# Eight scatters a sequence, each held until its predecessor has landed and five of them ahead of the first normalisation's GpSimd step

## The reference, cut to what matters

```python
x = x + L0_xattn(layernorm(x), ctx, ctx)      # 16 heads of 16, Wq Wk Wv Wo bo
x = x + L0_ffn(layernorm(x))                  # 16 experts, 4 a token, shared expert
x = x + L1_xattn(layernorm(x), ctx, mask)     # q k v with biases, masked keys
x = x + L1_ffn(layernorm(x))                  # 16 experts, 2 a token, shared expert
# L0_ffn of an input x (normalised):
scores = sigmoid(x @ gate_w.T)                # 4 experts of the 2 best groups of 4
y = sum over chosen e of cw[e] * (silu(x @ Wg[e].T) * (x @ Wu[e].T)) @ Wd[e].T
return x + y + shared(x)
```

## Time and profile before

| | us |
|---|---|
| median of three runs | 2772.32 |
| lowest and highest run | 2769.62 and 2779.53 |
| span of the profiled execution | 3211.6 |
| TensorE busy in it | 2501.5 (78%) |
| vector engine busy | 1619.2 (50%) |
| ScalarE busy | 1173.3 (37%) |
| GpSimd busy | 998.9 (31%) |

### The profile page before, as it was taken

How to read it: one execution, slowest core, us unless ns; L and a number is a source line. 1 busy time by engine, 2 the same in 40 slices (tenths; PEclk the granted TensorE clock), 3 DMA queues, 4 the chain that set the end, 5 groups by cost and what they waited for, 6 DMA issues and landing times.

```text
span 3211.6 us, 52941 instructions
## 1 busy us (share of the span) xinstructions
PE 2501.5 (78%) x16160; PEld 1935.5 (60%) x16161; DVE 1619.2 (50%) x5230; ACT 1173.3 (37%) x2564; POOL 998.9 (31%) x1104
## 2 busy tenths in 40 slices
PE   6888888888897499999768787788788877699400
PEld 4667676667676387778545565555556655587400
DVE  2655555556565344444336555455455545344333
ACT  3444444445353133333234434334343443233100
POOL 1232333332323500000134434434443442400366
PEclk9998989999898799999889889889898889899755
DMA  4111111111111544444431212211221120544465
GB/s 163 43 64 42 58 47 57 49 63 42 63 43 55 138 151 148 148 150 149 133 108 60 71 64 62 70 61 60 63 70 55 60 76 33 136 149 148 144 178 171
DMA packets 202635, 292.72 MB, mean 91 GB/s; under 512 B 30423, under 2 KB 151514, under 8 KB 202074
## 3 DMA queue, kind: packets, MB, share of 16 engines
q1 hardware_dynamic: 160522, 185.09, 18.0%
q0 software_dynamic: 37456, 102.81, 10.2%
q10 hardware_dynamic: 4608, 4.20, 0.9%
HBM read 155.65 MB, written 136.34 MB: 91 GB/s over the span
## 4 chain that ended last, share of the span: by engine, by line
PE 54%; another core or an unknown queue 12%; DVE 10%; issue 9%; ACT 8%; POOL 4%; DMA 3%; SPq 0%; DVEq 0%; POOLq 0%; ACTq 0%
PE ps L1358 12%; PE ps L1293 7%; PE ps L1366 6%; PE ps L1212 5%; PE ps L1193 4%; PE ps L1233 3%; ACT W L667 3%; POOL ygath L543 3%; PE ps L1371 3%; PE ps L1176 2%; DVE mxp L846 2%; PE ps L1281 2%; PE ps L1268 2%; PE ps L1377 1%
## 5 line engine op out<-in xcount | busy, mean ns | idle before, releaser
L510 POOL DMA_INDIRECT xsort<-xn,xidx x384 | 377.7, 984 | 570.7 <-DVE xidx L1050 467.8
L846 DVE TENSOR_REDUCE mxp<-ps 128x8 f32<-128x960 f32 x256 | 284.6, 1154 | 498.2 <-PE ps L1212 268.3
L1358 PE MATMUL ps<-wgu,ygath 128*128 x1664 | 440.6, 387 | 28.0 <-issue 23.3
L543 POOL DMA_INDIRECT ygath<-ysort,yidx x384 | 371.2, 967 | 152.3 <-issue 107.6
L1212 PE MATMUL ps<-KB,Q 64*128 64x240 f32 x2048 | 287.5, 428 | 100.7 <-DVE mxp L846 80.3
L1100 DVE TENSOR_TENSOR ygath<-ygath,ps 128x128 f32<-128x128 f32 x416 | 119.5, 287 | 441.6 <-ACT ygath L744 441.6
L667 ACT ACTIVATE W<-ps 120x1024 f32<-120x1024 f32 x256 | 249.6, 1034 | 239.8 <-remote 169.8
L1358 PEld LDWEIGHTS ps<-wgu,ygath 128*128 128x128 f32 x1664 | 284.9, 191 | 74.2 <-issue 52.2
L1212 PEld LDWEIGHTS ps<-KB,Q 64*128 64x128 f32 x2048 | 218.3, 218 | 165.7 <-DVE mxp L846 86.9
L1293 PE MATMUL ps<-W,wsgu 128*128 128x256 f32 x1024 | 290.7, 434 | 1.2 <-ACT th L691 1.2
L1193 PE MATMUL ps<-xnT,wq 128*128 128x256 f32 x1024 | 280.0, 422 | 10.8 <-ACT xnT L630 9.3
(11 more groups left out here) (160 smaller groups left out, 4027.9 us busy)
## 6 DMA issues: line engine op xcount, KB each, us to landing
ygath<-xsort SPq DMA_DIRECT2D x416, 128.0 KB, 2.0
ysort<-ygath SPq DMA_DIRECT2D x208, 256.0 KB, 2.3
based<-XO SPq DMA_DIRECT2D x64, 256.0 KB
XB<-in_x SPq DMA_DIRECT2D x32, 256.0 KB
wgu<-in_wgu SPq DMA_DIRECT2D x2, 4096.0 KB, 14.3
XB<-based SPq DMA_DIRECT2D x32, 256.0 KB
X<-based SPq DMA_DIRECT2D x32, 256.0 KB
out_x<-X SPq DMA_DIRECT2D x32, 256.0 KB
```

The lines of the kernel that those rows point to most:

```text
L510: e.indirect_dma_start(out=xsort, in_=xn2[s][:, t, :], in_offset=None, out_offset=bass.IndirectOffsetOnAxis(ap=xidx[s][:, t * 4 + k:t * 4 ...
L543: e.indirect_dma_start(out=ygath[s][:, t * 4 + k, :], out_offset=None, in_=ysort, in_offset=bass.IndirectOffsetOnAxis(ap=yidx[s][:, t * 4 ...
L846: ins = e.tensor_reduce(top[:, :, row:row + 2, :], ps[:, 4 * s + 2 * g:4 * s + 2 * g + 2, 0:4 * LK].rearrange("p t (i h k) -> p t i h k", ...
L1358: mm = e.matmul(ps[:, 2 + h, 0:2 * F], xtT[h][:, c, :], wgu[:, bass.ds(x * (DC * 2 * F) + c * 2 * F, 2 * F)], start=(c == 0), stop=(c == D ...
```

## The change

A new role `d` is the sequence whose scatter ended a half before; its eight scatters become eight steps `sc0` to `sc7`, and one more half is appended for GpSimd (`tail`). `sc0` waits for `slots` as the scatters did; each of the others waits until its predecessor's sixteen counts are there. Five stand ahead of `rstd1`, three between `rstd1` and `rstd2`; `xb` goes behind `rstd2`. Since `d` in one half is `c` of the half before, `sc0` stands where the burst stood. Layer 1 keeps its four scatters in one step; for it the tail half is empty.

```diff
-    "Pool0": "rstd1:n xb:n rstd2:b scatter:c",
+    "Pool0": "sc0:d sc1:d sc2:d sc3:d sc4:d rstd1:n sc5:d sc6:d sc7:d rstd2:b xb:n",
...
-def run_halves(e, engine, stages, lead=True):
+def run_halves(e, engine, stages, lead=True, tail=False):
...
         at_role = {"a": (u, s), "b": (u, 0) if s else (u - 1, 1), "c": (u - 1, s),
+                   "d": (u - 1, 0) if s else (u - 2, 1),
                    "n": (u + 1, 0) if s else (u, 1), "m": (u + 1, s)}
...
+    if tail:
+        half(NIT + 1, 0)
...
+                def scatter_piece(u, s, m):
+
+                    if m == 0:
+                        e.wait_ge(sig["slots", s], at("slots", L, u))
+                    else:
+                        e.wait_ge(sig["sc", s], at("sc", L, u, 16 * m))
+                    apart(e)
+                    scatter_one(s, m // 4, m % 4)
...
-                run_halves(e, f"Pool{L}", stages)
+                else:
+                    for m in range(8):
+                        stages[f"sc{m}"] = lambda u, s, m=m: scatter_piece(u, s, m)
+                run_halves(e, f"Pool{L}", stages, tail=True)
```

More of the change, by code:

```diff
@@ L505, in _, with scatter_one @@
             e.wait_ge(w_small, NSMALL)
[L507 to L514, removed]
+            def scatter_one(s, t, k):
+                e.indirect_dma_start(
+                    out=xsort, in_=xn2[s][:, t, :], in_offset=None,
+                    out_offset=bass.IndirectOffsetOnAxis(
+                        ap=xidx[s][:, t * 4 + k:t * 4 + k + 1], axis=0),
+                ).then_inc(sig["sc", s], 16)
             steps = [0]
@@ L569, in scatter_rows @@
                     apart(e)
-                    scatter(L, s)
+                    for t in range(QT):
+                        for k in range(TOPK[L]):
+                            scatter_one(s, t, k)
+                def scatter_piece(u, s, m):
[5 more added lines that the diff above has]
+                    scatter_one(s, m // 4, m % 4)
                 def gather_rows(u, s):
```

## The result

The changed kernel takes 3144.92 us (median of four runs, 3138.07 to 3149.28), the one before 2772.79 us (four runs, 2769.62 to 2779.53). The ratio is 1.132, with a 95% interval of 1.130 to 1.135: 372 us slower. The forecast was 3002 in a range to 3080: the right sign and the right loop, and 142 us too small.

What follows compares the result with a forecast made beforehand. It took landing waits to close a GpSimd and vector loop of 33.35 us a half against 25.86: 30 x 7.5 = 225, plus 5 at the stage's end, 2772 + 230 = 3002 us; range 2800 to 3080.

Steps and rivals of the forecast that it cites:

- What is the half of the kernel before in the runs?: Layer 0: the scatter stalls belong to the profiled execution only, so a half takes 25.86 us in the runs, not 32.45.
- The closed loop through rstd2 and shift2: Layer 0, L1050 to L1050 through eight scatters, rstd2, shift2 and place: 33.35 us a half against 25.86, +7.5 us.
- Rival A: The stall is in the runs too: half 32.45 us today, new loop 33.35, result 2804 us; chance 0.11.
- B: Faster: the stall is in the runs, spaced scatters no longer cause it, loop 28.9 us, result 2665 us; chance 0.11.
- C: Nothing moves because the waits are hidden, needing an interval under 1.93 us: 2772 us; chance 0.04.
- the scatters' part: GpSimd in layer 0: scatters start 3.0 us apart (2.36 to 3.5) in place of 1.27, with a landing of 2.2.
- the XL addition: GpSimd: moving xb behind rstd2 takes 1.27 us out of rstd2's way, worth nothing, its reader being two halves off.
- the way from shift2 to L1050: Vector engine in layer 0: from shift2's start through HS, choose, weigh and place to the end of L1050, 9.6 us.
- the stage's end: Sequences 30 and 31 scatter in series after the last halves; last landing at 1093.8 against release at 1089.2: +5 us.
- shift1 and rstd1, "costs nothing": rstd1, behind five scatters, comes 14.7 us after L1050, some 2 us late for shift1; ve2 still precedes rstd2 by 6 us.
- ScalarE's xn2, "Nothing more": xn2 waits for the eighth landing, 24.0 us, about when shift2 is done (23.9), so it adds nothing.
- The signs: Scatters 3.0 us apart, shift2 idling 5 us or more as largest vector wait, halves 33 to 34, GpSimd's chain share above 4%.

Runs made afterwards that it cites:

- the second profile: The kernel before, unchanged, run and profiled once more: 2772.45 us, ratio 0.999, with a profiled span of 2770.2 us.

## Why the prediction was right and wrong

*What is the half of the kernel before in the runs?* Right. The choice of 25.86 us against 32.45, made from the gap between the profile and the runs and from one early half, was the largest; measured 25.75. In this half TensorE is the bound, busy for 25.12 of 25.99 us. The prediction argued from the budget that the stalls belong to the profiled execution alone; the second profile shows it.

*The closed loop through rstd2 and shift2.* Right, and shown from three sides: without waits it is gone (2780), with rstd1 in it as well it is 2 us longer (3188), and with one wait, short enough to stay under TensorE's 25.75 us, it costs nothing (2780). With rstd2 moved ahead the loop closes through ScalarE's wait for the eighth landing instead (3145). What all the slow ones share are the landings in series. Rival A and B rested on a stall that the runs do not have; C is excluded by the result.

*The sum.* Wrong, +230 for +372 us, though the mechanism was right. The step that failed is the pricing of the loop and of the stage's end: the scatters' part, at 3.0 us an interval, was too short, the XL addition was put at nothing, the way from shift2 to L1050 was taken as the vector engine's alone, and the end was put at +5. By terms, in the profiles of the changed kernel and the second of the kernel before, whose spans differ by 366 us:

- The scatters from first start to rstd2's start: 22.21 forecast, 24.16 and 23.69 in the two halves shown, 24.06 in the mean. The landing is 2.4 us, not the 2.2 between the rows' ends, and the first two scatters are 4.1 and 3.6 us apart, 3.9 in the mean. SyncE issues the store of base and the next loads in that time (366.77 to 368.33 in the first half shown); that they are the cause is not shown. 1.85 x 30 = 55.5 us.
- The XL addition, costed at nothing "since its reader is two halves off". The reader was looked at, and not what runs on the vector engine in the same microsecond. 1.07 x 30 = 32 us, and 37.5 measured by taking it away.
- From shift2 to L1050, 9.6 forecast: 10.89 and 11.65 in the two halves shown, which is 9.8 and 10.6 with the hold taken off. The mean half of 36.92 leaves 36.92 - 33.35 - 1.85 - 1.07 = 0.65 us for this, 19.5 us. It is the vector engine's wait for rank: ahead of L1058 it idles 0.29 and 0.94 us in the two halves, and 0.66 in the mean against 0.07 in the second profile of the kernel before. Rank is late behind SH, whose eight matmuls take 3.12 us to the start of Q0 in the first half shown and 1.73 in the kernel before. The rows behind this list show TensorE's clock there.
- The end of the stage: +5 forecast, +25.5 measured. The forecast put the sixteen intervals at 3.0 us each and overlooked that this kernel's fills and tables are written beside them, of which the earlier trace rows had a sign: one scatter's landing of 15.57 us there. Two landings of 9.31 and 9.62 us in place of 2.4 are 14 us of the difference. Where none of the last sixteen scatters waits for a landing, the end is back at 33.6 us, with the same fills and tables.
- The half of before, 25.75 and not 25.86, adds 3. Together 55.5 + 32 + 19.5 + 20.5 + 3 = 130.5 of the missing 136.

For the third term, the stretches of SH and behind it, with the columns of the earlier trace rows (the granted clock is the figure before the last two), in the changed kernel's two halves:

```profile
394.60:396.60 2.00, 1.94 (x7) 1.79 (x8) 1.62 (x13) 1.72 (x4) 0.00 (x0) 0.50 0.00 0
...
398.90:400.60 1.70, 1.70 (x14) 1.41 (x12) 1.44 (x7) 1.70 (x3) 0.00 (x0) 1.00 0.00 0
...
432.80:434.90 2.10, 2.10 (x6) 1.65 (x6) 1.69 (x13) 2.10 (x8) 0.00 (x0) 0.50 0.00 0
```

and SH's in the second profile of the kernel before:

```profile
330.30:332.20 1.90, 1.90 (x12) 1.70 (x11) 1.52 (x12) 1.61 (x5) 0.00 (x0) 1.00 0.00 0
```

TensorE idles 7.62 and 7.57 us for ScalarE's xn2 and V ahead of its transposes in the two halves, and SH then runs at a granted clock of 0.50, the lower of its two levels; in the kernel before it runs at 1.00. So the term comes from the new wait itself, by the path over TensorE that the forecast left out. No run separates the clock from that path's own length.

*shift1 and rstd1, "costs nothing".* Right: rstd1 is done about 16 us after L1065 where 14.7 was forecast, and the chain passes it and shift1 by.

*ScalarE's xn2, "Nothing more".* Right for the changed kernel, but only just: with rstd2 moved forward, or with the XL addition out of shift2's way, this wait takes over at once.

*The signs.* Scatters 3.17 us apart for 3.0, and 7.15 us of idling ahead of shift2, agree. A half is 36.9 us and not 33 to 34. The wait for rstd2, 408 us in all, is the vector engine's second largest and not its largest (L1115 in the expert stages has 469). GpSimd's share of the chain went to 8%, but it is 7% in the second profile of the kernel before, so the 4% of the first was no base for a sign.

*The profiled execution, 3244 forecast.* Wrong by its premise that a profile would stall again: it was 3136.2.

*The range.* Its upper end, 3080, cut off the case of an interval of 3.5 us, 3114, that the text itself had worked out; even that did not hold the result, as it had only the one unknown in it and neither the hold nor the stage's end.

*The landing and the hold.* The Trainium skill's page "DMA: Bandwidth & Descriptors", section "Anatomy of one DMA — SWDGE (gpsimd) path", has a fixed and a size-dependent part, from which 2.3 us for a landing of 128 KB is an estimate; the median measured is 2.4, and the page was nearer than the prediction's 2.2. The Trainium skill's page "SBUF — State Buffer", section "Who interferes with whom", was weighed for one of its sentences only. Another there says that a VectorE operation with two SBUF inputs contends with a GpSimd operation that reads SBUF, and the section calls their shared ports an exclusive lock. The trace agrees: L837, with two such inputs, takes 1.22 us beside L561's 1.25 us and 0.16 without it. This was the rule that bore on the move of the XL addition.

## What to carry to other kernels

Here a wait for a landing cost nothing as long as the loop that it closed stayed under the pace of the busiest engine. So write the loop out before placing it, from semaphore to semaphore and over all engines, and add up its length. Between that length and the pace lies all the room there is: here about 1 us with one wait of seven, none with three. Then ask what the new idle time will do to the engines behind it: here TensorE came back from its wait at the lower clock in both halves shown. And ask what else runs in the same microsecond as a step of the loop. At the end of this stage nothing covered such waits, and beside other traffic two landings took over 9 us.

If a profile is much longer than the runs, take a second one before reading the first: here one profiled execution of two was 439 us longer than every run.

## What was not expected of the hardware

An operation of 128 x 2 numbers on the vector engine took 1.22 us in place of 0.16 when GpSimd's 128 x 512 addition had started 0.05 us before it. A landing took 2.4 us in nearly all places, but 9.3 and 9.6 us beside the zero fills and the table writes. And in one profiled execution the vector engine's first maxima started some 4.5 us after the modelled end of TensorE's matmuls (366.84 against 362.34 in the earlier trace rows), behind nearly every burst of scatters, in both layers, while in all eleven other profiles layer 1's halves took 25.5 to 25.7 us with the same code.
